# A mixture-of-experts layer that scatters widened token rows into expert order, lets the experts scatter their results, and moves the shared expert forward

## The chip, the cores and the metric

One core of one Trainium2 chip. The time is the device time of one launch, in microseconds, of the slowest (here the only) core; it is compared as the median of several runs. Beside the runs there is one profiled execution with a trace.

## The reference, cut to what matters

A two-layer transformer on 2 x 1024 tokens of 256 features, float32. Layer 0 is attention (16 heads) and a quantized gated feed-forward; layer 1 is retention (4 heads) and a mixture of experts, and only the latter is changed in what it does:

```python
router_logits = x @ gate_w.T
probs = jax.nn.softmax(router_logits, axis=-1)
topk_w, topk_idx = jax.lax.top_k(probs, K)            # E = 64 experts, K = 6, inner width 176
topk_w = topk_w / jnp.sum(topk_w, axis=-1, keepdims=True)
h = jax.nn.silu(jnp.einsum('th,eih->tei', x, experts_w1))
y = jnp.einsum('tei,ehi->teh', h, experts_w2)
routed_out = jnp.einsum('teh,te->th', y, combine)     # combine: the six weights, zero elsewhere
g, u = jnp.split(x @ shared_gate_up.T, 2, axis=-1)
shared_out = jax.nn.silu(g) * u @ shared_down.T       # inner width 352
return (routed_out + shared_out).reshape(orig_shape)
```

after which comes x = layernorm(x + ffn(x)).

## The kernel before, in words

The program is a row of blocks, each closed by a barrier of all engines: `attend`, `out_ffn` (output projection, feed-forward of layer 0, and on SyncE the weights and tables of the retention), `retention`, then `route`, `experts` and `combine`. Inside a block each engine has its own instruction stream, and semaphores order them. A stream is run in its written order, so an instruction that waits holds everything behind it on its engine.

`route`. `keep_x` holds the 2048 tokens as 16 tiles of 128 tokens, `keep_x_t` the transposed copy. TensorE makes the logits; VectorE takes the eight best, forms the six weights, counts tokens by expert, and gives each of the 12,288 (token, choice) pairs a slot in an array of 160 tiles of 128 slots, in which each expert begins a new tile (`slot_i`, L1563). SyncE copies `keep_x` to `x_rows` in HBM. Then the slots are inverted: for each of 96 (tile, choice) pairs VectorE and GpSimd make one-hot matrices (L1573 to L1576, L1458) and TensorE adds up their product (L1490), and the sum is `tok_i`, the token of each slot (L1581). A slot that no pair has comes out as token 0. `owner` is the expert of each tile (for tiles past the last used one the last expert).

`experts`. For each of the 160 tiles: GpSimd gathers 128 rows of 1 KB from `x_rows` by `tok_i` (L1624, ten buffers); SyncE loads the tile's expert (`exp_w`, 2 x 176 KB, six buffers); TensorE transposes the rows (L1638), ScalarE copies them (L1678), TensorE multiplies by the first weights (L1649), ScalarE applies silu (L1685), TensorE multiplies by the second (L1658), VectorE copies the result out (L1713), and ScalarE's queue writes the tile to `y_rows` (L1690), in slot order.

`combine`. For each token tile and choice GpSimd gathers 128 rows of `y_rows` by `slot_i` (L1757, 12 buffers), and VectorE adds them to `keep_x`, each times its weight (L1822). Meanwhile the shared expert is computed (L1773 on TensorE, L1801, L1812, L1783), its result is added (L612), and the layer norm follows in four chunks of four tiles (L620 to L640), each then stored to `out`.

## Time and profile before

| | |
|---|---|
| median of 3 runs | 1465.17 us (1461.19 to 1465.23) |
| the profiled execution, its own time | 1456.11 us |
| its span, first to last instruction | 1454.4 us |
| TensorE busy | 1185.9 us (82%) |
| VectorE busy | 818.7 us (56%) |
| GpSimd busy | 550.8 us (38%) |
| ScalarE busy | 520.6 us (36%) |
| DMA moved | 154.78 MB, mean 106 GB/s |

The shares are over the whole span, over stages with different limits; the blocks concerned begin at about 822 us (`route`), 936 us (`experts`) and 1299 us (`combine`) of the span. The time outside the span is 1.7 us. The profiled execution was 9 us shorter than the median of the runs.

### The profile page before, as it was taken

To read this page: it belongs to the slowest core of one execution; us is meant where nothing else is said; L and a number is where in the kernel's file an instruction comes from. 1 tells how busy PE (TensorE), PEld (TensorE's weight loads), DVE (VectorE), ACT (ScalarE), POOL (GpSimd) and SP (SyncE) were. 2 spreads that over 40 slices of the span, in tenths; PEclk is the share of its full clock that TensorE was granted. 3 is DMA by queue.
4 is the path that set the end of the run, shared out by engine and by line. 5 is a ranking of instruction groups with operands and counts; after the bars stand their busy time and mean duration, and the time that the engine had idled before them with its cause. 6 is when DMAs were issued, how large, how long until landed. Compare 5 with 4: busy or idle time off the path is not lost. (4 is left out here: it accounts for less than half of the span.)

```text
span 1454.4 us, 19589 instructions
## 1 busy us (share of the span) xinstructions
PE 1185.9 (82%) x6248; PEld 689.2 (47%) x6287; DVE 818.7 (56%) x1572; ACT 520.6 (36%) x1052; POOL 550.8 (38%) x564
## 2 busy tenths in 40 slices
PE   5589999999999699989997515699999997778641
PEld 2242222222222255665455511188888886664321
DVE  6499999999997565333446379712221221114554
ACT  1137777777778432101234100033333332221000
POOL 6002447663536500012110105454444443314775
PEclk9799999999999889989998755589999999888855
DMA  4960531443101400000000100199999999962343
GB/s 133 182 151 8 91 46 21 52 58 45 21 10 16 166 2 1 0 1 1 1 1 1 60 0 1 33 295 303 313 306 305 308 302 231 220 192 57 101 127 97
DMA packets 142584, 154.78 MB, mean 106 GB/s; under 512 B 50674, under 2 KB 111443, under 8 KB 142419
## 3 DMA queue, kind: packets, MB, share of 16 engines
q1 hardware_dynamic: 106882, 98.71, 26.9%
q0 software_dynamic: 12288, 33.57, 9.2%
q10 hardware_dynamic: 23312, 21.24, 4.5%
q8 instruction: 52, 0.85, 0.3%
q14 instruction: 50, 0.40, 0.1%
HBM read 118.34 MB, written 32.51 MB: 104 GB/s over the span
## 5 line engine op out<-in xcount | busy, mean ns | idle before, releaser
L495 ACT ACTIVATE l_ret_store<-attn_st 128x512 f32<-128x512 f32 x512 | 280.0, 598 | 103.5 <-PE attn_st L406 87.3
L519 DVE TENSOR_REDUCE attn_neg<-attn_mx 128x8 f32<-128x1024 f32 x256 | 299.1, 1202 | 13.0 <-PE attn_mx L386 12.1
L1713 DVE COPY exp_y_sb<-exp_y_ps 128x256 f32<-128x256 f32 x160 | 68.0, 425 | 288.7 <-PE exp_y_ps L1658 288.7
L1624 POOL DMA_INDIRECT exp_rows<-x_rows,moe_tok_i x160 | 150.9, 943 | 189.2 <-PE exp_xt_ps L1638 172.6
L1649 PE MATMUL exp_h_ps<-exp_xt,exp_w 128*88 128x128 f32 x1280 | 174.2, 281 | 23.2 <-DMA exp_w<-in_w 22.8
L386 PE MATMUL attn_mx<-attn_k_st,attn_q_st 96*128 96x512 bf16 x512 | 154.9, 384 | 17.8 <-DVE attn_neg L519 15.1
L1658 PE MATMUL exp_y_ps<-exp_w,exp_ht 96*128 96x256 f32 x640 | 167.9, 385 | 0.0
L1649 PEld LDWEIGHTS exp_h_ps<-exp_xt,exp_w 128*88 128x88 f32 x1280 | 150.3, 161 | 32.2 <-DMA exp_w<-in_w 31.1
L406 PE MATMUL attn_st<-attn_q_st,attn_k_st 128*128 128x512 bf16 x473 | 160.0, 383 | 5.3 <-ACT l_ret_store L495 2.3
L418 PE MATMUL attn_o<-l_ret_store,l_ret_tab 128*32 128x512 f32 x1024 | 136.4, 604 | 2.8 <-ACT l_ret_store L495 0.8
L1678 ACT ACTIVATE exp_xt<-exp_xt_ps 128x256 f32<-128x256 f32 x160 | 61.5, 384 | 210.4 <-PE exp_xt_ps L1638 206.8
L406 PEld LDWEIGHTS attn_st<-attn_q_st,attn_k_st 128*128 128x128 bf16 x512 | 48.1, 97 | 157.2 <-ACT l_ret_store L495 114.6
L1757 POOL DMA_INDIRECT comb_got<-y_rows,moe_slot_i x96 | 92.6, 965 | 78.3 <-POOLq L58 33.1
L1658 PEld LDWEIGHTS exp_y_ps<-exp_w,exp_ht 96*128 96x128 f32 x640 | 110.9, 193 | 9.2
L1685 ACT ACTIVATE exp_ht<-exp_h_ps 88x256 f32<-88x256 f32 x160 | 60.8, 380 | 114.6 <-PE exp_h_ps L1649 114.6
L278 POOL CAST attn_neg_parts<-attn_neg 128x128 bf16<-128x128 f32 x16 | 4.6, 290 | 209.1 <-DVE attn_neg L519 209.1
L386 PEld LDWEIGHTS attn_mx<-attn_k_st,attn_q_st 96*128 96x128 bf16 x512 | 48.5, 98 | 67.6 <-DVE attn_neg L519 29.5
L1822 DVE SCALAR_TENSOR_TENSOR keep_x<-comb_got,moe_weight,keep_x 128x256 f32<-128x256 f32 x96 | 46.6, 486 | 42.4 <-DMA comb_got<-y_rows,moe_slot_i 38.9
L1638 PE MATMUL exp_xt_ps<-keep_ident,exp_rows 128*128 128x128 f32 x320 | 63.1, 279 | 6.8 <-DVE exp_w L1708 6.0
L1490 PE MATMUL route_m<-route_hot_high,route_hot_low 128*128 128x320 bf16 x96 | 42.2, 447 | 26.8 <-DVE route_hot_high L1576 22.1
L354 PE MATMUL attn_st<-keep_x_t,l0b_front 128*128 128x512 f32 x64 | 37.1, 741 | 32.4 <-DVE l0b_front L505 25.1
L1783 PE MATMUL comb_y<-comb_w_down,comb_sh_h 128*128 128x256 f32 (+1 forms) x96 | 33.8, 510 | 35.4 <-DVE keep_x L612 35.4
(233 smaller groups left out, 1643.9 us busy)
## 6 DMA issues: line engine op xcount, KB each, us to landing
exp_w<-in_w SPq DMA_DIRECT2D x320, 176.0 KB
y_rows<-exp_y_sb ACTq DMA_DIRECT2D x160, 128.0 KB, 6.2
parts<-l0b_front SPq DMA_DIRECT2D x32, 192.0 KB, 11.3
attn_k_st<-parts SPq DMA_DIRECT2D x48, 128.0 KB, 7.2
attn_q_st<-parts SPq DMA_DIRECT2D x48, 128.0 KB, 7.9
l_ret_tab<-in_tables SPq DMA_DIRECT2D x4, 1024.0 KB
exp_rows<-x_rows,moe_tok_i POOLq DMA_INDIRECT x160, 6.3
keep_x_t<-in_x_t SPq DMA_DIRECT2D x4, 512.0 KB
```

What stands on the lines that cost most here:

```text
L386: mm = pe.matmul(bank[:, half * CH:(half + 1) * CH], q, k_st[g % BUFS][0:STACK, h, half * CH:(half + 1) * CH], start=True, stop=True)
L406: pe.matmul(st_ps[n % BANKS][:], k_st[g % BUFS][:, h, kt * P:(kt + 1) * P], q_st[g % BUFS][:, h, c * CH:(c + 1) * CH], start=True, stop=Tr ...
L418: mm = pe.matmul(o_ps[32 * h:32 * h + 32, :], v_st[:, b, kt, head + h], probs[s % 2][:, h], start=True, stop=True)
L495: act.activation(probs[s % 2][:, h], st_ps[n % BANKS][:], ACT.Exp, scale=SCALE0).then_inc(exp_done, 1)
L519: dve.tensor_reduce(neg[m % 2][:, i], mx_ps[slot["score", n] % 2][:].rearrange("p (j k) -> p j k", k=P), AX.X, ALU.max, negate=True).then_ ...
L1624: pool.indirect_dma_start(rows[b % RB][:], None, a["x_rows"], bass.IndirectOffsetOnAxis(ap=tok_i[:, b:b + 1], axis=0)).then_inc(rows_in[b ...
L1638: mm = pe.transpose(xt_ps[b % 2][:, k * P:(k + 1) * P], rows[b % RB][:, k * P:(k + 1) * P], ident[:])
L1649: mm = pe.matmul(h_ps[b % 2][0:HALF, j * P:(j + 1) * P], w1[n][:, k, j], xt[b % 2][:, k], start=(k == 0), stop=(k == KT - 1))
L1658: mm = pe.matmul(y_ps[b % 2][:, 0:E], ht[b % 2][:, j], w2[b % B][:, j], start=(j == 0), stop=(j == 1))
L1678: act.activation(xt[b % 2][:], xt_ps[b % 2][:, 0:KT * P].rearrange("p (k t) -> p k t", k=KT), ACT.Copy).then_inc(xt_in, 1)
L1713: dve.tensor_copy(y_sb[b % YB][:], y_ps[b % 2][:, 0:E]).then_inc(y_in, 1)
L1757: pool.indirect_dma_start(got[n % B][:], None, a["y_rows"], bass.IndirectOffsetOnAxis(ap=slot_i[:, t, k:k + 1], axis=0)).then_inc(got_in[n ...
```

## The change

`keep_x` gets rows of 276 numbers, 1104 bytes: the token's 256 features (`x` is a view of them), its number, its six slots, its six weights, six constants k x 2048 and one unused. What each block does now:

- `out_ffn`: GpSimd fills `pad`, a row that carries a token number far out of bounds and slots of -1, and SyncE writes it to all 20,480 rows of `xs` in HBM, in 8 transfers, behind the loads for the retention; the block ends only when they have landed.
- `route`: the one-hot products and `tok_i` are gone, and so is the copy to `x_rows`. GpSimd scatters each token tile's wide rows to `xs` once for each choice, by `slot_i`, 96 indirect transfers of 128 rows of 1104 bytes, and waits for all. The shared expert is computed here, on TensorE behind the slot arithmetic, and left in `moe_shared`.
- `experts`: the rows of a tile are contiguous in `xs`, and ScalarE's queue loads them (12 buffers, 11 tiles ahead). For each four tiles VectorE finds in the rows which of the six slots is this one (`aim`: four small operations), and from that the weight of the row and the row of `y_rows` that it goes to: choice x 2048 + token. VectorE multiplies by the weight as it copies the result out of PSUM, and GpSimd scatters 128 rows of 1 KB to `y_rows`; padding rows have a destination out of bounds and are not written. For the first 16 tiles VectorE also adds `moe_shared` to `keep_x`.
- `combine`: SyncE loads for each token tile its six rows a token, 768 KB in one plain transfer, 8 buffers. For even tiles VectorE adds them in halves; for odd ones TensorE does, as six products with the identity into one PSUM bank. No weights and no gathers are left.

The diff, cut to its core:

```diff
@@ out_ffn
+            sp.wait_ge(padded, 3)
+            for i in range(PAD_PARTS):
+                sp.dma_start(a["xs"].rearrange("(b p) n -> p b n", p=P)[:, i * PER_PAD:(i + 1) * PER_PAD],
+                             pad[:].unsqueeze(1).to_broadcast([P, PER_PAD, XW])).then_inc(pad_out, 16)
+            sp.wait_ge(pad_out, 16 * PAD_PARTS)
@@ route, SyncE
-            sp.dma_start(a["x_rows"].rearrange("(t p) n -> p t n", p=P), x[:]).then_inc(x_out, 16)
+            sp.dma_start(w_up[:], a["w_sh_up"].rearrange("(k p) n -> p k n", p=P)).then_inc(sh_in, 16)
...
@@ route, GpSimd
-            pool.wait_ge(split, 1)
-            for n, (t, k) in list(enumerate(pairs))[1::2]:
...
-                pool.tensor_scalar(hot_low[:, n % HOTS], iota[:, 0:P], low[:, t, k:k + 1], None,
-                                   ALU.is_equal).then_inc(hot_low_in, 1)
+            pool.wait_ge(slotted, 1)
+            for t, k in pairs:
+                pool.indirect_dma_start(a["xs"], bass.IndirectOffsetOnAxis(ap=slot_i[:, t, k:k + 1], axis=0),
+                                        wide[:, t], None, bounds_check=TILES * P - 1, oob_is_err=False
+                                        ).then_inc(rows_out, 16)
+            pool.wait_ge(rows_out, 16 * len(pairs))
@@ route, TensorE
-            for n, (t, k) in enumerate(pairs):
...
+            for c in range(NCH + 1):
+                if c < NCH:
+                    for m in range(ST):
+                        shared_up(c * ST + m)
+                if c >= 1:
+                    for t in range((c - 1) * TC, c * TC):
+                        shared_down(t)
@@ route, VectorE
+            dve.tensor_copy(slot_i[:], slot).then_inc(slotted, 1)
+            for n in range(NCH * ST):
...
+                dve.tensor_tensor(sh_h[c % 2][0:rows, m], u_ps[n % 2][0:rows, :], sh_gate[n % 2][0:rows],
+                                  ALU.mult).then_inc(fuse, 1)
@@ experts, GpSimd
-                pool.indirect_dma_start(rows[b % RB][:], None, a["x_rows"], bass.IndirectOffsetOnAxis(
-                    ap=tok_i[:, b:b + 1], axis=0)).then_inc(rows_in[b % RB], 16)
+                pool.wait_ge(y_in, b + 1)
+                pool.wait_ge(aimed, b // SET + 1)
+                pool.indirect_dma_start(a["y_rows"], bass.IndirectOffsetOnAxis(
+                    ap=dst_i[b // SET % 6][:, b % SET:b % SET + 1], axis=0), y_sb[b % YB][:], None,
+                    bounds_check=TOP * TOK - 1, oob_is_err=False).then_inc(y_out[b % YB], 16)
@@ experts, ScalarE
-                act.dma_start(a["y_rows"].rearrange("(t p) n -> t p n", p=P)[b], y_sb[b % YB][:]
-                              ).then_inc(y_out[b % YB], 16)
+                act.dma_start(rows[:, b % RB], a["xs"].rearrange("(b p) n -> b p n", p=P)[b]
+                              ).then_inc(rows_in[b % RB], 16)
@@ experts, VectorE
+                if b % SET == 1 and b // SET + 1 < TILES // SET:
+                    aim(b // SET + 1)
+                if b < NT:
+                    dve.tensor_tensor(x[:, b], x[:, b], shared[:, b], ALU.add).then_inc(shared_in, 1)
...
-                dve.tensor_copy(y_sb[b % YB][:], y_ps[b % 2][:, 0:E]).then_inc(y_in, 1)
+                dve.tensor_scalar(y_sb[b % YB][:], y_ps[b % 2][:, 0:E], weight[b // SET % 4][:, b % SET, 0:1], None,
+                                  ALU.mult).then_inc(y_in, 1)
@@ combine, SyncE
+            for t in range(NT):
+                if t >= B:
+                    sp.wait_ge(norm["summed"], t - B + 1)
+                sp.dma_start(got[t % B][:], a["y_rows"].rearrange("(k t p) n -> t p k n", k=TOP, p=P)[t]
+                             ).then_inc(got_in[t % B], 16)
@@ combine, TensorE
+            for t in range(1, NT, 2):
+                pe.wait_ge(got_in[t % B], 16 * (t // B + 1))
+                if t >= 5:
+                    pe.wait_ge(norm["summed"], t - 3)
+                for k in range(TOP):
+                    mm = pe.matmul(y_ps[t // 2 % 2][:, 0:E], keep["ident"][:], got[t % B][:, k],
+                                   start=(k == 0), stop=(k == TOP - 1))
+                mm.then_inc(made, 1)
@@ combine, VectorE
+            def sum_rows(t):
+                n, rows = t // 2, got[t % B]
+                dve.wait_ge(got_in[t % B], 16 * (t // B + 1))
+                dve.tensor_tensor(rows[:, 0:3], rows[:, 0:3], rows[:, 3:6], ALU.add).then_inc(halved, 1)
+                dve.wait_ge(halved, n + 1)
+                dve.tensor_tensor(rows[:, 0], rows[:, 0], rows[:, 1], ALU.add).then_inc(paired, 1)
+                dve.tensor_tensor(x[:, t], x[:, t], rows[:, 2], ALU.add).then_inc(thirds, 1)
...
```

GpSimd's own stream from the end of `route` to the end of the program, before (line, operation, what it writes and reads, shape, count):

```order
L1453 MEMSET route_sums 128x64
L1458 TENSOR_SCALAR route_hot_low<-route_iota,route_low 128x128 x48
L1624 DMA exp_rows<-x_rows,moe_tok_i 128x256 x160
L1757 DMA comb_got<-y_rows,moe_slot_i 128x256 x48
```

and the same stream of the changed kernel:

```order
L1479 MEMSET route_sums 128x64
L1482 DMA xs<-keep_x,route_slot_i 20480x276 x96
L1679 IOTA exp_mine 128x160
L1684 DMA y_rows<-exp_y_sb,exp_dst_i 12288x256 x160
L648 TENSOR_TENSOR comb_ln_rstd<-comb_ln_var,keep_neg_half 128x4 x4
```

The 96 indirect transfers have moved from `combine` (where they were gathers, 48 of them in the row shown and 48 more behind it) to `route`, where they are scatters; the 160 of `experts` have turned from gathers ahead of the tile to scatters behind it.

ScalarE's stream in `experts`, in the steady state before (silu, then the write of the tile two back):

```order
L1678 ACTIVATE exp_xt<-exp_xt_ps 128x256
L1685 ACTIVATE exp_ht<-exp_h_ps 88x256
L1690 DMA y_rows<-exp_y_sb 128x256
```

and of the changed kernel, from the start of the block:

```order
L1738 DMA exp_rows<-xs 128x276 x11
L1745 ACTIVATE exp_xt<-exp_xt_ps 128x256 x2
L1738 DMA exp_rows<-xs 128x276
L1752 ACTIVATE exp_ht<-exp_h_ps 88x256
```

Eleven loads now stand ahead of ScalarE's first copy, and in each tile the transfer stands between the copy and the silu instead of behind the silu.

## Rows read from the trace of the kernel before

**Rows 1.** The windows view by stage: busy us of each engine, granted clock, DMA.

```profile
core 0: us, PE busy (x) PEld busy (x) DVE busy (x) ACT busy (x) POOL busy (x), PEclk, DMA share, GB/s
...
884.00:936.00 52.00, 42.16 (x96) 9.94 (x96) 50.18 (x245) 0.00 (x0) 29.34 (x48) 0.50 0.00 1
...
1040.00:1080.00 40.00, 39.83 (x281) 35.94 (x280) 8.49 (x20) 15.24 (x40) 18.82 (x20) 1.00 0.98 306
...
1200.00:1240.00 40.00, 29.34 (x188) 25.26 (x186) 5.95 (x14) 10.65 (x28) 13.17 (x14) 0.96 1.00 229
...
1380.00:1420.00 40.00, 16.52 (x40) 9.96 (x40) 23.90 (x64) 0.59 (x1) 30.64 (x33) 0.59 0.44 127
```

**Rows 2.** VectorE's copies of the experts' results in the timeline: first, 121st, last.

```profile
951.51 0.42 DVE L1713 COPY exp_y_sb<-exp_y_ps 128x256 f32<-128x256 f32 x1 [11.93 <-PE exp_y_ps L1658]
...
1195.98 0.42 DVE L1713 COPY exp_y_sb<-exp_y_ps 128x256 f32<-128x256 f32 x1 [1.53 <-PE exp_y_ps L1658]
1197.94 0.42 DVE L1713 COPY exp_y_sb<-exp_y_ps 128x256 f32<-128x256 f32 x1 [1.54 <-PE exp_y_ps L1658]
...
1295.85 0.42 DVE L1713 COPY exp_y_sb<-exp_y_ps 128x256 f32<-128x256 f32 x1 [0.44 <-PE exp_y_ps L1658]
```

**Rows 3.** DMA queues, 936 to 1190 us: q1 weights, q0 gathers, q10 writes.

```profile
q1 hardware_dynamic: 29424, 43.64, 53.4%
q0 software_dynamic: 6155, 16.82, 23.0%
```

**Rows 4.** The same queues, 1245 to 1290 us.

```profile
q1 hardware_dynamic: 4392, 6.52, 48.3%
q0 software_dynamic: 528, 1.44, 24.2%
```

**Rows 5.** The timeline of GpSimd's gathers in `combine`: the first two and the last.

```profile
1299.76 0.94 POOL L1757 DMA_INDIRECT comb_got<-y_rows,moe_slot_i  x1 [33.07 <-POOLq L58]
1301.00 0.94 POOL L1757 DMA_INDIRECT comb_got<-y_rows,moe_slot_i  x1 [0.30 <-issue]
...
1438.81 0.95 POOL L1757 DMA_INDIRECT comb_got<-y_rows,moe_slot_i  x1 [0.30 <-issue]
```

**Rows 6.** DMA issues of 1340 to 1440 us: KB each, median us to landing.

```profile
comb_got<-y_rows,moe_slot_i POOLq DMA_INDIRECT x77, 2.8
```

**Rows 7.** The timeline of `route`'s end: start us, us, what, idle before it.

```profile
883.05 0.21 DVE L1563 CAST moe_slot_i<-route_slot 128x96 int32<-128x96 f32 x1
...
934.40 0.24 DVE L1581 CAST moe_tok_i<-route_tok_f 128x160 int32<-128x160 f32 x1
935.79 0.55 DVE L1708 MEMSET exp_ht<- 96x256 f32 x2 [1.14 <-PEq L58]
```

**Rows 8.** Groups of `combine` by line: busy us, mean ns, idle before.

```profile
L1783 PE MATMUL comb_y<-comb_w_down,comb_sh_h 128*128 128x256 f32 (+1 forms) x96 | 33.8, 510 | 35.4 <-DVE keep_x L612 35.4
L1773 PE MATMUL comb_g<-keep_x_t,comb_w_up 128*128 128x512 f32 (+1 forms) x48 | 26.4, 677 | 10.6 <-DMA comb_w_down<-in_w_sh_down 10.6
L1773 PE MATMUL comb_u<-keep_x_t,comb_w_up 128*128 128x512 f32 (+1 forms) x48 | 25.1, 649 | 7.3 <-DVE comb_sh_h L1812 7.3
```

**Rows 9.** DMA in 820 to 833 us, GB/s of 40 slices, and its issue.

```profile
GB/s 0 0 0 0 0 0 0 0 0 0 0 214 190 331 337 336 329 331 337 350 356 353 350 353 347 353 350 350 347 350 328 47 25 25 19 0 0 0 0 0
...
x_rows<-keep_x SPq DMA_DIRECT2D x1, 2048.0 KB
```

**Rows 10.** DMA in 490 to 640 us, 40 slices of 3.75 us, GB/s.

```profile
GB/s 143 271 372 416 392 18 4 0 0 0 0 0 0 4 0 0 0 0 0 0 4 0 0 0 2 0 0 0 4 0 0 0 0 0 0 4 0 0 0 0
```

**Rows 11.** Groups of 833 to 884 us: VectorE on 128x1024 float32.

```profile
L1561 DVE TENSOR_TENSOR route_pick<-route_place,route_chosen 128x1024 f32<-128x1024 f32 x6 | 7.4, 1226 | 0.2
```

**Rows 12.** The timeline of `combine`'s end, and a pair of its sums on TensorE.

```profile
1427.51 2.93 PE L1783 MATMUL comb_y<-comb_w_down,comb_sh_h 128*128 128x256 f32 x6 [4.17 <-DVE keep_x L612]
...
1442.10 0.42 DVE L612 TENSOR_TENSOR keep_x<-comb_y,keep_x 128x256 f32<-128x256 f32 x1
1442.44 1.39 DVE L620 BATCH_NORM_STATS2 comb_ln_stats<-keep_x 128x6 f32<-128x256 f32 x4
```

316 lines of the change are left out of this document (154 added, 162 removed).

## The prediction

> **What bounds the kernel now.** I first read the windows view by stage [rows 1]. No one engine bounds the three blocks that change. At the end of `route` (884 to 936 us) VectorE is busy 50.18 of 52 us and TensorE 42.16: they build and multiply the one-hot matrices. In `experts` TensorE is busy 39.8 of 40 us at the full clock while the DMA share is 0.98 at 306 GB/s, so two resources run out almost together. From 1200 us the rate falls: 14 tiles in 40 us instead of 20, TensorE 29.3 busy, DMA share 1.00 but only 229 GB/s. In `combine` GpSimd has the largest share, 30.64 of 40 us, at a DMA share of 0.44.
>
> Then the tile rhythm of `experts` in the timeline [rows 2]. The usual step from one result to the next is 1.96 us, which is TensorE's own pace. The first 120 steps take (1195.98 - 951.51) = 244.5 us, 2.04 each; the last 39 take 99.9 us, 2.56 each. The queues tell why. In the steady part the gathers hold 23.0% of 16 engines for 254 us for 16.82 MB [rows 3], 57 ns for each 1 KB row; in 1245 to 1290 us 24.2% of 16 x 45 us for 1.44 MB [rows 4], 124 ns for each. The weights cost 50 and 53 ns a KB. So only the gathers are slow there. What the late tiles have in common is that no token belongs to them: 12,288 pairs fill about 130 of 160 tiles, and each empty slot gathers token 0. I take 128 reads of one row as the cause of the late stalls.
>
> Last, `combine` [rows 5]: gathers start 1.25 us apart (0.94 us of GpSimd and 0.30 between), 96 of them from 1299.76 to 1438.81; a transfer lands 2.8 us after its issue [rows 6]. The loop is GpSimd's issue rate, with 17 us of start-up in which it waits for the shared expert.
>
> **`route`: what goes and what comes.** The slots are ready at 883.05 + 0.21 = 883.3 us, and `experts` begins at 935.8 [rows 7]; 52.5 us lie between. In their place stand 96 scatters on GpSimd. No scatter is in the trace. The nearest row is the gather: the same engine, the same 128 indices, the same count of rows, so 1.25 us each. I take it: 883.4 + 95 x 1.25 + 0.95 = 1003.1, the last lands some 2 us later, and 1.15 us of barrier as in [rows 7] follow. `experts` begins at about 1006: **70 us later**. The lower bound is an issue without the gap, 0.95 us each, 29 us less. The upper bound is a scatter that has to land before the next is issued, 1.25 + 2.8 us, 270 us more. I stay near the gather, and allow it up to 0.2 us more for the bounds test and the 1104-byte row, 19 us.
>
> Beside it runs the shared expert. Its matmuls were busy 33.8 + 26.4 + 25.1 = 85.3 us [rows 8], part of it at the low clock. TensorE can start when the slots' base is known, and VectorE joins at 883.3, so it ends by about 883 + 85 + 10 for the single output bank = 978, under the scatters. It costs nothing, but if the scatters were cheaper than 1.0 us each it would be the bound: without that cover the block would still be 43 us longer.
>
> **`out_ffn`.** The padding rows are 20,480 x 1104 B = 22.6 MB. A 2 MB store of 1 KB rows ran at about 345 GB/s [rows 9], so 66 us. They queue behind loads that end near 512 us, and from then to 640 the DMA engines move nothing [rows 10]: they are done at about 580, and the block has 60 us to spare. The three small fills ahead of GpSimd's first product cost under 1 us where its next norm waits anyway. Zero; uncovered it would be 66 us.
>
> **`experts`.** Bytes a tile before: 352 KB weights + 128 gathered + 128 written = 608 KB, at 306 GB/s 2.03 us, just the 2.04 of the first 120 steps. Now: 352 + 138 loaded + 12,288 / 130 = 94 rows written, 94 KB = 584 KB, 1.95 us, and TensorE needs 1.96. Late tiles: 352 + 138 KB from distinct addresses and nothing written, 1.6 us, so TensorE's 1.96. Both movements go in one direction. I keep a few stalls and take 1.98 us for all 159 steps: 314.8 against 344.3 us, **29 us less**. The bounds: 1.96 gives 33 less; tail or stalls unchanged gives 5 to 0 less.
> On the other engines a tile has slack. GpSimd's scatter of 0.94 us needs only `y_in`. VectorE's copy is 0.42 us in 1.96; the four small operations of `aim` come once in four tiles, and the addition of 0.42 us in 16 tiles. What they could delay is the copy out of a PSUM bank that has a twin. ScalarE issued one transfer a tile and still does, but its load is ahead of the silu, which `down` waits for; the copy ahead of it ends over 1 us before `up` does, so 0.33 us fits. `aim` waits for rows up to six tiles on, loaded 11 ahead. If it waited, VectorE's copies, then `y_ps`, then TensorE would be held.
>
> **`combine`.** It lasted 1454.4 - 1295.85 = 158.6 us from the last copy [rows 2]. Now 16 loads of 786 KB, 12.6 MB; at the 340 GB/s of a run of 1 KB rows [rows 9] 37 us, and 1.5 MB of stores among them 4.5 us. VectorE per pair: three rows at 3/4 of 1.23 us [rows 11] = 0.95, two additions and two norm additions of at most 0.42, with waits 2.6 us; with the norm of four tiles 8.4 us for four tiles, under the 10.6 of their transfers. So DMA sets the pace. Ahead of it: the last scatter and the barrier 4.5 us, the first transfer 2. Behind: six products at the low clock 2.93 us and their wait 3.2 us, then 1442.10 to 1454.4 unchanged, 12.3 us [rows 12]. Sum 4.5 + 2 + 37 + 4.5 + 3.2 + 12.3 = 63.5: **95 us less**. If VectorE were the bound it would be 34 for 41.5, 103 less.
> One thing speaks against 340 GB/s. A token's six rows lie 2 MiB apart, and the only rows in this trace with an address pattern that collides cost 124 instead of 57 ns [rows 3, 4]. At 2.2 times, the loads take 81 us, 44 more. The Trainium skill (DMA: Bandwidth & Descriptors, Latency and other measured facts) gives 164 GB/s where each partition's row is 2 MiB from the next, an estimate of 77 us for the loads; here the partitions' rows are adjacent and only the six blocks lie so far apart, which no row shows. [...]
>
> **Sum.** +70 - 29 - 95 = -54 us. The profiled execution had 1454.4 us of span and 1.7 around it, so 1402 by its measure; it was 9 us below the median of the runs, and against 1465.17 the same difference gives **1411 us**.
>
> **The rivals.**
> *A, the scatter is dear and the kernel slower.* One price decides: 54 us / 96 = 0.56, so from 1.81 us a scatter nothing is gained, and at 2.05 us it is 1434 + 54 = 1488. For it: the row is written, not read, is longer, and a bounds test is new. Against: the number of rows to describe is the same, and the DMA share is 0.35 to 0.44 during gathers, so there is room. A chance of 0.10.
> *B, the late tiles stay slow.* Then the stalls come from the repeated weights of the last expert, not from the gathers, and 25 us stay: 1436. Against: 50 to 53 ns a KB for weights. 0.08.
> *C, the loads of `combine` collide,* +44: 1455, faster by 0.7% still. 0.08.
> *D, the new order holds TensorE in `experts`* (rows late for `aim`, or ScalarE's transfer ahead of the silu): 0.2 us a tile is 32 us, 1443. For it: SyncE's issues there sometimes take longer. 0.10.
> *E, the change does not do what it says:* scatters cheaper by the gap, with the shared expert as bound, 1385. 0.04.
>
> **How the numbers follow.** The forecast, 1395 to 1427 with its own bounds (the 19 us of a slightly dearer scatter above, exact 1.96 and VectorE's pace below), has 0.60. The range goes up to take in B and D: 1394 to 1448. Faster, same and slower are parted at 0.3% of the time, about what a measurement of this kernel can tell. A is split into 0.02 near no change and 0.08 above; the rest is faster: 0.90, 0.02, 0.08.
>
> **What would show it.** GpSimd's scatters in `route` 1.25 us apart, near 883 to 1003, with the shared expert finished before them; steps of 1.96 us in `experts` up to the last tile; loads in `combine` landing 2.3 to 2.6 us apart with VectorE waiting for them. A scatter of 1.8 us, a shared expert that ends last, or VectorE waiting for rows in `experts` would make me wrong.

## The result and the profile after

The changed kernel takes 1472.91 us (median of 20 runs, 1467.42 to 1478.41), the kernel before beside it 1467.03 us (20 runs, 1460.09 to 1480.38). The ratio is 1.0044, its 95% interval 1.0027 to 1.0061: slower by 0.4%, where I had forecast 1411 us, 3.7% faster. The profiled execution took 1476.08 us, its span 1474.4.

The windows view of the changed kernel, in the columns of [rows 1]; first the end of `route` in three parts, then `experts`, then `combine`:

```profile
core 0: us, PE busy (x) PEld busy (x) DVE busy (x) ACT busy (x) POOL busy (x), PEclk, DMA share, GB/s
884.00:950.00 66.00, 36.55 (x78) 16.71 (x79) 3.90 (x6) 4.47 (x9) 50.19 (x52) 0.74 0.30 108
950.00:1010.00 60.00, 4.02 (x12) 2.46 (x10) 1.38 (x2) 1.57 (x3) 43.43 (x45) 0.55 0.30 108
1010.00:1051.00 41.00, 29.00 (x84) 17.05 (x84) 2.07 (x3) 6.00 (x14) 0.00 (x0) 0.82 0.00 0
1100.00:1140.00 40.00, 39.75 (x276) 35.45 (x277) 12.72 (x40) 14.94 (x40) 18.47 (x19) 1.00 0.95 291
1240.00:1280.00 40.00, 38.63 (x258) 33.01 (x258) 12.24 (x39) 13.90 (x37) 18.43 (x19) 1.00 0.95 274
1420.00:1460.00 40.00, 24.34 (x84) 18.88 (x84) 23.50 (x67) 0.00 (x0) 4.16 (x3) 0.78 1.02 328
```

The second line is the surprise: from 950 to 1010 us GpSimd issues scatters, and all other engines stand still, TensorE with 4.02 us of work in 60. In the third line the scatters are over and the shared expert is still being computed.

The timeline of GpSimd's scatters and of the barrier behind them, which answers to [rows 5, 7]:

```profile
884.25 1.24 POOL L1482 DMA_INDIRECT xs<-keep_x,route_slot_i  x1 [58.13 <-DVE route_slot_i L1623]
885.80 0.97 POOL L1482 DMA_INDIRECT xs<-keep_x,route_slot_i  x1 [0.30 <-issue]
...
1005.88 0.97 POOL L1482 DMA_INDIRECT xs<-keep_x,route_slot_i  x1 [0.30 <-issue]
...
1050.08 0.38 ACT L1562 ACTIVATE moe_shared<-route_y 128x256 f32<-128x256 f32 x1 [1.65 <-PE route_y L1529]
...
1051.41 0.55 DVE L1792 MEMSET exp_ht<- 96x256 f32 x2 [16.21 <-PEq L74]
```

The scatters are as forecast, 1.28 us apart (0.97 and 0.30), 884.3 to 1006.9 us. But `experts` begins at 1051.4, 45 us after the 1006 of the forecast, behind ScalarE's last copy of the shared expert.

Why that was late shows in the timeline of TensorE, ScalarE and VectorE beside the scatters:

```profile
899.57 0.38 ACT L1562 ACTIVATE moe_shared<-route_y 128x256 f32<-128x256 f32 x1 [2.42 <-PE route_y L1529]
...
911.55 2.93 PE L1529 MATMUL route_y<-route_w_down,route_sh_h 128*128 128x256 f32 x6 [6.83 <-issue]
914.27 2.46 PE L1519 MATMUL route_g<-keep_x_t,route_w_up 128*128 128x512 f32 x4
916.56 1.88 PE L1519 MATMUL route_u<-keep_x_t,route_w_up 128*128 128x512 f32 x4
...
923.03 0.38 ACT L1562 ACTIVATE moe_shared<-route_y 128x256 f32<-128x256 f32 x1 [11.53 <-remote]
934.23 0.60 ACT L1558 ACTIVATE route_sh_gate<-route_g 128x512 f32<-128x512 f32 x1 [10.82 <-issue]
934.88 3.73 PE L1519 MATMUL route_g<-keep_x_t,route_w_up 128*96 128x512 f32 x4 [13.00 <-issue]
945.43 0.69 DVE L1631 TENSOR_TENSOR route_sh_h<-route_u,route_sh_gate 128x512 f32<-128x512 f32 x1 [46.46 <-DMA parts<-l0b_front]
...
1006.33 0.38 ACT L1562 ACTIVATE moe_shared<-route_y 128x256 f32<-128x256 f32 x1 [26.71 <-remote]
```

Read them crosswise. TensorE's output tile of 911.55 is complete by 914.5; ScalarE, which waits for nothing else, takes it at 923.03. The gate product of 914.27 is complete by 916.7 and taken at 934.23, the up product of 916.56 by 918.4 and taken at 945.43. The profile models the end of a product, but the trace also records when a semaphore rises. For the gate product that ended at 896.52, ahead of these, that is 896.54; for the output tile that ended at 914.48 it is 923.00, and for the gate product that ended at 920.16 it is 956.61. So it is not ScalarE that wakes up late: TensorE's completion signals arrive one at a time, 11.2 us apart, and further and further behind the work. In the other direction nothing is late: TensorE goes on at 934.88, right behind ScalarE's 934.23 + 0.60. The releasers named ("remote", a DMA of a much earlier block) are old semaphore events: none of them is what was waited for. The queues don't explain it, since the DMA share is 0.30.

The experts' results on VectorE (which answer to [rows 2]) and the queues of 250 us in `experts` (q1 weights, q10 rows, q0 scatters, to [rows 3]):

```profile
1067.10 0.48 DVE L1803 TENSOR_SCALAR exp_y_sb<-exp_y_ps,exp_weight 128x256 f32<-128x256 f32 x1 [10.63 <-PE exp_y_ps L1719]
...
1329.62 0.48 DVE L1803 TENSOR_SCALAR exp_y_sb<-exp_y_ps,exp_weight 128x256 f32<-128x256 f32 x1 [2.54 <-PE exp_y_ps L1719]
...
1409.60 0.48 DVE L1803 TENSOR_SCALAR exp_y_sb<-exp_y_ps,exp_weight 128x256 f32<-128x256 f32 x1 [0.38 <-PE exp_y_ps L1719]
```

```profile
q1 hardware_dynamic: 27829, 41.28, 57.3%
q10 hardware_dynamic: 16448, 16.15, 22.3%
q0 software_dynamic: 5413, 11.18, 13.8%
```

The last 39 steps take 80.0 us instead of 99.9, and no step over 3.3 us is left: the tail came out as forecast. The first 120 take 262.5 us, 2.19 each, instead of the 244.5 of before and the 1.98 of the forecast.

Last, `combine`: DMA in 1420 to 1462 us and the timeline of its edges, which answer to [rows 9, 12]:

```profile
GB/s 15 146 361 379 359 347 351 347 349 347 348 347 349 349 347 355 346 352 349 347 347 348 352 349 348 346 350 347 347 348 350 346 349 364 384 386 296 46 301 208
```

```profile
1411.27 0.97 POOL L1684 DMA_INDIRECT y_rows<-exp_y_sb,exp_dst_i  x1 [0.30 <-issue]
1419.84 8.17 SPq L1826 DMA_DIRECT2D comb_got<-y_rows  x6
1424.80 0.96 DVE L1858 TENSOR_TENSOR comb_got<-comb_got 128x768 f32<-128x768 f32 x1 [14.72 <-DMA comb_got<-y_rows]
...
1465.46 0.42 DVE L628 TENSOR_TENSOR keep_x<-comb_y,keep_x 128x256 f32<-128x256 f32 x1 [1.68 <-PE comb_y L1849]
```

It runs at the DMA rate, 347 GB/s, and takes 1474.4 - 1409.6 = 64.8 us, where 63.5 was forecast.

### The profile page after: what moved, and what is told of

Read it like the earlier page. It is cut to its first block and busy times, and to the rows that moved or that the text cites. A ratio compares the mean times of both kernels' runs of the same rounds, so it can differ in the third digit from the quotient of the medians.

```text
span 1474.4 us, 20063 instructions
## 1 busy us (share of the span) xinstructions
PE 1176.9 (80%) x6287; PEld 693.5 (47%) x6287; DVE 776.3 (53%) x1429; ACT 526.0 (36%) x1068; POOL 530.1 (36%) x522
## 5 line engine op out<-in xcount | busy, mean ns | idle before, releaser
L1684 POOL DMA_INDIRECT y_rows<-exp_y_sb,exp_dst_i x160 | 156.3, 977 | 204.4 <-DVE exp_y_sb L1803 82.4
L1803 DVE TENSOR_SCALAR exp_y_sb<-exp_y_ps,exp_weight 128x256 f32<-128x256 f32 x160 | 77.4, 484 | 241.2 <-PE exp_y_ps L1719 166.8
L422 PE MATMUL attn_st<-attn_q_st,attn_k_st 128*128 128x512 bf16 x512 | 173.5, 383 | 2.9 <-ACT l_ret_store L511 2.1
L402 PE MATMUL attn_mx<-attn_k_st,attn_q_st 96*128 96x512 bf16 x512 | 154.9, 384 | 15.6 <-DVE attn_neg L535 15.3
L1719 PE MATMUL exp_y_ps<-exp_w,exp_ht 96*128 96x256 f32 x640 | 164.6, 379 | 0.4 <-ACT exp_ht L1752 0.4
L1710 PEld LDWEIGHTS exp_h_ps<-exp_xt,exp_w 128*88 128x88 f32 x1280 | 145.5, 158 | 38.5 <-DMA exp_w<-in_w 26.8
L1482 POOL DMA_INDIRECT xs<-keep_x,route_slot_i x96 | 93.6, 975 | 87.1 <-DVE route_slot_i L1623 58.1
L1529 PE MATMUL route_y<-route_w_down,route_sh_h 128*128 128x256 f32 (+1 forms) x96 | 30.2, 459 | 75.9 <-issue 62.5
L1631 DVE TENSOR_TENSOR route_sh_h<-route_u,route_sh_gate 128x512 f32<-128x512 f32 (+1 forms) x12 | 8.2, 688 | 143.9 <-DMA parts<-l0b_front 89.9
L1082 PE MATMUL ret_a<-keep_x_t,l_ret_store 128*128 128x512 f32 x128 | 59.5, 618 | 2.4 <-PEq L74 2.4
```

The source lines that it names most:

```text
L402: mm = pe.matmul(bank[:, half * CH:(half + 1) * CH], q, k_st[g % BUFS][0:STACK, h, half * CH:(half + 1) * CH], start=True, stop=True)
L422: pe.matmul(st_ps[n % BANKS][:], k_st[g % BUFS][:, h, kt * P:(kt + 1) * P], q_st[g % BUFS][:, h, c * CH:(c + 1) * CH], start=True, stop=Tr ...
L1482: pool.indirect_dma_start(a["xs"], bass.IndirectOffsetOnAxis(ap=slot_i[:, t, k:k + 1], axis=0), wide[:, t], None, bounds_check=TILES * P - ...
L1684: pool.indirect_dma_start(a["y_rows"], bass.IndirectOffsetOnAxis(ap=dst_i[b // SET % 6][:, b % SET:b % SET + 1], axis=0), y_sb[b % YB][:], ...
L1710: mm = pe.matmul(h_ps[b % 2][0:HALF, j * P:(j + 1) * P], w1[n][:, k, j], xt[b % 2][:, k], start=(k == 0), stop=(k == KT - 1))
L1719: mm = pe.matmul(y_ps[b % 2][:, 0:E], ht[b % 2][:, j], w2[b % B][:, j], start=(j == 0), stop=(j == 1))
```

## The experiments

All edits are to the changed kernel unless said otherwise. Runs of one group had the same chip. "Indirect" means the last scatter's end in `route`, "shared" the shared expert's last copy, "experts" that block's first instruction, all in us of the span; "steps" are the mean of the first 120 steps of `experts`, and the sum of the last 39; "before" is the kernel before on that chip. All columns are of one execution each, but for the last two of e10_pause and e5b_lockstep: there the times are medians of 6 and 8 executions, beside 13 of the kernel before. These spread over 7.7, 5.5 and 15.0 us, so a difference between two single times can be trusted only if it is larger.

| run | indirect | shared | experts | steps | kernel | before |
|---|---|---|---|---|---|---|
| profile after | 1006.9 | 1050.5 | 1051.4 | 2.19, 80.0 | 1476.1 | |
| e1_throttle | 1009.9 | 1056.2 | 1057.2 | 2.14, 77.1 | 1472.2 | 1471.5 |
| e2_after | 1008.3 | 1085.2 | 1086.1 | 2.17, 80.2 | 1507.2 | |
| e3_aligned | 1008.8 | 1053.5 | 1054.5 | 2.16, 78.5 | 1471.8 | |
| e4_owner | 1011.2 | 1057.0 | 1057.9 | 2.15, 82.1 | 1478.5 | |
| e5_lockstep | 1017.2 | 950.5 | 1027.7 | 2.13, 79.2 | 1442.9 | 1451.9 |
| e6_gather | 1138.2 | 952.3 | 1150.2 | 2.17, 80.4 | 1573.8 | |
| e7_drain | 1034.4 | 954.4 | 1044.9 | 2.12, 79.6 | 1459.2 | |
| x4_direct | 1010.9 | 953.3 | 1021.4 | 2.17, 82.0 | 1444.3 | |
| c0_before | | | | 2.07, 96.4 | 1475.3 | 1472.4 |
| c1_after | 1008.8 | 1055.7 | 1056.7 | 2.14, 77.9 | 1472.4 | |
| x1_nowrite | 1009.5 | 1056.0 | 1057.0 | 2.09, 80.7 | 1468.7 | |
| e8_loose | 1020.5 | 987.2 | 1031.0 | 2.13, 77.1 | 1444.8 | |
| c2_after | 1009.6 | 1055.6 | 1056.6 | 2.15, 80.0 | 1474.6 | 1465.2 |
| x4b_direct | 1008.3 | 1051.3 | 1052.2 | 2.16, 79.9 | 1470.7 | |
| e6b_gather | 1136.1 | 1168.6 | 1169.8 | 2.15, 79.1 | 1589.2 | |
| e9_tight | 1019.5 | 969.5 | 1030.1 | 2.17, 78.5 | 1450.0 | |
| e10_pause | 1017.9 | 950.5 | 1028.4 | 2.13, 80.4 | 1446.4 | 1469.3 |
| e5b_lockstep | 1026.9 | 980.8 | 1037.4 | 2.17, 78.0 | 1458.5 | |

### First group: how many scatters are outstanding, and the experts' rows

```diff
+                if n >= 4:
+                    pool.wait_ge(rows_out[n % 4], 16 * (n // 4))
```

> Edit: of the route's 96 scatters at most four are outstanding (GpSimd waits for scatter n-4 before it issues scatter n). In the changed kernel's profile the scatters run from 884.2 to 1005.9 us, one every 1.28 us, and from 903 us on TensorE's completion signals reach ScalarE and VectorE one by one, 11.2 us apart, so that the block ends at 1051.3 us. Theory 1 (what holds the signals back is the number of scatters that are outstanding, or that GpSimd's sequencer has run ahead and its queue is full): no signal is late, the shared expert ends by about 960 us, the block ends 5 to 10 us behind the last scatter, at 1010 to 1020 us, and the whole kernel takes 1435 to 1445 us. Theory 2 (each scatter holds signals back by itself, however many are outstanding): the signals stay about 11 us apart and the block ends at 1045 to 1060 us. Rival (the chip needs the depth): the scatters themselves slow down to 2 us or more each and the block ends after 1070 us.

The block ended at 1057.2 us and the signals came 11.2 and 22.4 us apart as before. The scatters kept their 1.28 us: four were hardly ever outstanding in the unlimited loop either (in x4_direct below one lands 2.5 us after its issue). Theory 1 fell: the signals are late although no more than four transfers are under way.

```diff
             pe.wait_ge(sh_in, 16 * (1 + ST))
+            pe.wait_ge(rows_out, 16 * len(pairs))
```

> Edit: TensorE starts the shared expert only when all 96 scatters have landed. Theory (scatters and the shared expert disturb each other, alone each is as quick as its rows say): the scatters end at 1006 us as before the edit, the shared expert then takes 24 groups of four matmuls at 1.72 us and 16 output tiles at 2.04 us, about 74 us, with no late signal, and the block ends near 1081 us; the kernel takes about 30 us more than the changed one. Rival (the shared expert is slow by itself, since its operands or its weights are slow to read): signals are late after 1006 us too and the block ends after 1120 us.

The shared expert alone took 1008.3 to 1085.2, 77 us, with no late signal, and the scatters alone were no quicker than beside it. The two disturb each other in one direction: the scatters hold up the shared expert.

```diff
+PITCH = 320
-    a["xs"] = nc.dram_tensor("xs", (TILES * P, XW), F32, kind="Internal").ap()
+    a["xs"] = nc.dram_tensor("xs", (TILES * P, PITCH), F32, kind="Internal").ap()
```

> Edit: the widened rows lie 1280 bytes apart in HBM instead of 1104, so that each begins at a multiple of 256 bytes; as many bytes are moved as before, and the scatters of the route have no bounds check. Theory A (the experts' 160 steps of 2.15 us instead of 1.98 come from reads of 1104-byte rows that begin anywhere, which take 61 ns each): the rows' reads fall below 55 ns each and the experts take 335 to 345 us from their first instruction to the last copy instead of 358. Theory B (the queue of the weights is what the tiles wait for, at 55 ns a kilobyte, whatever the rows' place): the experts take 355 to 361 us. The route doesn't change by more than 3 us by either.

First to last copy of the experts' results took 337.6 us, which lies among the 334.2 of e1_throttle and the 340.4 of e2_after on the same chip, with untouched experts. Where a row begins makes no difference that these runs can tell.

```diff
+            chain(dve.tensor_scalar(spare[:], owner_f[:], float(EXPERTS), None, ALU.is_ge))
+            chain(dve.tensor_scalar(other[:], tile_no[:], float(-TILES), None, ALU.add))
...
+            chain(dve.tensor_tensor(owner_f[:], owner_f[:], other[:], ALU.add))
```

> Edit: the tiles behind the last one in use name experts 0, 1, 2 ... as their owners instead of all naming the last expert, so that no tile reads the weights that its neighbour has just read; their rows are pads, so nothing else changes. Theory of the forecast's second rival (weights of one expert read again and again are slow): the queue of the weights takes less than 57 ns a kilobyte in the tail instead of 58.9, and the experts end 5 us or more earlier. Theory B (all reads compete for the same bandwidth, wherever they lie): no difference over 3 us in the experts' time of 358.2 us.

The last 39 steps took 82.1 us, the longest of the group. Weights that are read again and again aren't slow; what rival B wanted as a cause isn't there in the changed kernel.

### Second group: signals paced, gathers, pauses, direct stores

```diff
+                if n >= 4 and n % 2 == 0 and 9 + n // 2 < len(signals):
+                    pool.wait_ge(*signals[9 + n // 2])
```

> Edit: from the fifth scatter on, before every second scatter, GpSimd waits for TensorE's next completion signal of the shared expert (29 of its 40 signals, one behind the other), so that no signal can fall more than two scatters behind; behind scatter 60 the rest run unhindered. With four outstanding scatters the signals were as late as without a limit, so it isn't the number outstanding. Theory 3 (TensorE's signal loses to GpSimd's stream of scatters and passes as soon as GpSimd pauses): the shared expert ends by about 970 us, the scatters end between 1010 and 1025 us, the block by 1030 us, and the kernel takes 1445 to 1455 us. Rival (a signal needs 11.2 us once the stream has begun, whether GpSimd pauses or not): 29 signals at up to 11 us make the block end after 1100 us.

```diff
+            for n, (t, k) in enumerate(pairs):
+                if n >= RD:
+                    pool.wait_ge(read_in[n % RD], 16 * (n // RD))
+                pool.indirect_dma_start(read[:, n % RD], None, a["xs"], bass.IndirectOffsetOnAxis(
...
```

> Edit: ahead of its 96 scatters GpSimd issues 96 gathers by the same indices, of the same rows of 1104 bytes, from the rows' array into 24 spare buffers; the shared expert has its place, so it now runs beside the gathers. Theory 4 (the late signals belong to scatters, that is to indirect transfers that write HBM): the shared expert runs at its pace beside the gathers and ends near 945 us; the gathers end near 1008 us, the scatters near 1132 us, and the block right behind them. Theory 3 (any stream of indirect transfers at this pace does it): the signals come 11 us apart beside the gathers too, and again beside the scatters, so that the shared expert has not ended by 1050 us.

```diff
+                if n and n % 8 == 0:
+                    pool.wait_ge(rows_out, 16 * n)
```

> Edit: after every eight scatters GpSimd waits until all that it has issued have landed, then goes on: eleven pauses of about 2 us. Theory 3 (a signal passes as soon as GpSimd pauses, and the stream has to run some 20 us before signals are late at all): the shared expert ends by 960 us, the scatters near 1030 us, the block with them, and the kernel takes 1450 to 1460 us. Rival (the lateness has nothing to do with the stream's breaks): signals stay 11.2 us apart and the block ends after 1065 us.

```diff
-                pool.indirect_dma_start(a["y_rows"], bass.IndirectOffsetOnAxis(
...
+                pool.dma_start(a["y_rows"].rearrange("(t p) n -> t p n", p=P)[b % (TOP * NT)], y_sb[b % YB][:]
+                               ).then_inc(y_out[b % YB], 16)
```

> Edit in the experts, which leaves out the scatter of the results: each tile's 128 rows of 1 KB are stored in order by one direct transfer from GpSimd's queue, pads too, as in the kernel before. Its output is not that of the reference. Theory C (the scatter of 1 KB rows to places all over 12 MB is what makes all queues slower per kilobyte, 55 ns for the weights instead of 49.7): the weights' queue falls to 51 ns a kilobyte or less, and the experts take 335 to 345 us from their first instruction to the last copy instead of 358.2. Theory D (the rows' direct reads, or the bytes as a whole, do it): the experts take 350 to 365 us.

None of the four had a late signal, and each seemed to bear a theory out. But x4_direct has the route of the changed kernel, word for word, and was free of them too: its shared expert ended at 953.3 us, its block at 1021.4. This was a chip on which the kernel before takes 1451.9 us. The group tells nothing about signals without a control. It does show the route undisturbed: behind the last scatter `experts` still begins 10.5 us later, not 3. In the trace's records of GpSimd 7.9 us of that are the drain that ends its block. On the experts, theory C fell: with direct stores the first 120 steps took 2.17 us, with scatters in the other three 2.12 to 2.17.

### Third group: the controls

> The kernel before, unchanged, profiled on the same chip as the three below, since its time differs by 20 us from chip to chip (1471.5 us beside the first four runs, 1451.9 us beside the next four), and the profiles of before and after weren't necessarily taken on one. If the experts' steps of the kernel before are quicker than those of the changed one on one chip too, by 0.1 us or more, then the change itself slows them; if both have steps of about the same length, the difference in the two profiles lay in the chips.

> The changed kernel, unchanged, as the control that the last four runs lacked: one of them had the route of the changed kernel word for word, and still its shared expert ended at 953 us with no late signal and its block at 1021 us. Theory 5 (the late signals belong to the program: its layout or its timing): this run shows them again, the shared expert ends at 1045 to 1057 us and the experts begin behind it. Theory 6 (they depend on the chip or the execution): this run may show none, the shared expert then ends near 953 us, the block near 1021 us, and the kernel takes about 30 us less than in its first profile, beside before.

The late signals were back in c1_after (shared expert ended at 1055.7 us). And they were in the kernel before as well: in its `combine`, which took 172.0 us here from the last copy instead of 158.6. The timeline of c0_before there, TensorE and ScalarE:

```profile
1353.54 1.88 PE L1773 MATMUL comb_g<-keep_x_t,comb_w_up 128*96 128x512 f32 x4
1353.65 0.60 ACT L1801 ACTIVATE comb_sh_gate<-comb_g 128x512 f32<-128x512 f32 x1 [4.47 <-DMA y_rows<-exp_y_sb]
...
1370.45 0.59 ACT L1801 ACTIVATE comb_sh_gate<-comb_g 96x512 f32<-96x512 f32 x1 [16.20 <-DMA y_rows<-exp_y_sb]
```

The product of 1353.54 is complete by 1355.4 and taken at 1370.45, 16.8 us after the one ahead of it. GpSimd's gathers ran from 1336.5 to 1366.5 there. The profile of before that I had read has a longer stretch without a pause, 36 gathers from 1331.3 to 1376.9 us, and no late signal in it; 42 us into it ScalarE still takes a product as it ends:

```profile
1371.91 1.88 PE L1773 MATMUL comb_g<-keep_x_t,comb_w_up 128*128 128x512 f32 x4
1373.83 0.60 ACT L1801 ACTIVATE comb_sh_gate<-comb_g 128x512 f32<-128x512 f32 x1 [2.84 <-PE comb_g L1773]
```

The queues of 250 us, c0_before from 952 us, 4.5 ahead of its first copy (q0 gathers, q10 stores), and c1_after from its first copy (q10 rows, q0 scatters):

```profile
q1 hardware_dynamic: 28929, 42.92, 53.9%
q0 software_dynamic: 5768, 15.76, 22.9%
q10 hardware_dynamic: 16750, 15.25, 18.9%
```

```profile
q1 hardware_dynamic: 28337, 42.04, 57.7%
q10 hardware_dynamic: 16707, 16.41, 22.5%
q0 software_dynamic: 5536, 11.37, 13.9%
```

```diff
-                    bounds_check=TOP * TOK - 1, oob_is_err=False
+                    bounds_check=0, oob_is_err=False
```

> Edit in the experts: the bounds of the result scatter are set so low that all rows but those for place 0 are dropped; the array is filled with zeros earlier, beside the pads. The output is not that of the reference. Theory E (weights, rows and results compete for one bandwidth, and what is above 1.96 us a step is the weights' lateness): without the 44 MB/s-class writes, 11.2 MB in 254 us, the steps fall to 1.96 to 2.03 us, and the experts take 320 to 330 us from first to last copy. Rival (reads alone are the limit, writes are free): the steps stay at 2.10 us or more and they take 334 us or more.

The queues of x1_nowrite, 250 us from the first copy, in which nearly nothing is written:

```profile
q1 hardware_dynamic: 28958, 42.95, 66.6%
q10 hardware_dynamic: 17103, 16.79, 24.5%
q0 software_dynamic: 5667, 0.07, 1.5%
```

Add the reads: 42.92 + 15.76 = 58.7 MB in c0_before, 42.04 + 16.41 = 58.5 in c1_after, 42.95 + 16.79 = 59.7 in x1_nowrite, 235, 234 and 239 GB/s, while 15.3, 11.4 and 0.1 MB were written. Taking all writes away gives 0.05 us a step; the steps of 2.09 us and the 331.6 us from first to last copy lie between what theory E and its rival wanted, the steps nearer to the rival. So it isn't the sum of both directions that sets the pace. That the bytes read set it is argued and not shown: a tile reads the same bytes in any of these kernels but for 10 KB, so like steps give like read rates whatever the cause, and reads alone run at 347 GB/s in `combine`. (The expectation's 11.2 MB in 254 us are 44 GB/s, not MB/s.)

```diff
+                if n >= 12 and n % 2 == 0 and 4 + n // 2 < len(signals):
+                    pool.wait_ge(*signals[4 + n // 2])
```

> Edit: as with the signals waited for one by one before every second scatter, but beginning at scatter 12 and seven signals behind, so that no wait holds unless a signal is really late. If the chip or execution shows late signals in the unchanged kernel here, this kernel shows whether such a bound is enough: shared expert ended by 970 us, last scatter by 1012 us, block by 1023 us. If the unchanged kernel has no late signals either, this one's route ends within 2 us of that one's.

Here one sees how a pause works. The timeline of e8_loose:

```profile
943.29 1.88 PE L1526 MATMUL route_u<-keep_x_t,route_w_up 128*128 128x512 f32 x4
943.85 0.97 POOL L1489 DMA_INDIRECT xs<-keep_x,route_slot_i  x1 [0.30 <-issue]
946.65 0.60 ACT L1565 ACTIVATE route_sh_gate<-route_g 128x512 f32<-128x512 f32 x1 [5.28 <-DMA parts<-l0b_front]
947.30 1.96 PE L1526 MATMUL route_g<-keep_x_t,route_w_up 128*96 128x512 f32 x4 [2.13 <-ACT route_sh_gate L1565]
947.40 0.97 POOL L1489 DMA_INDIRECT xs<-keep_x,route_slot_i  x1 [2.58 <-DMA parts<-l0b_front]
948.67 0.97 POOL L1489 DMA_INDIRECT xs<-keep_x,route_slot_i  x1 [0.30 <-issue]
948.80 0.69 DVE L1638 TENSOR_TENSOR route_sh_h<-route_u,route_sh_gate 128x512 f32<-128x512 f32 x1 [20.70 <-DMA parts<-l0b_front]
```

GpSimd stops at 944.8 for a signal that is late. Within 1.9 us ScalarE has its own, and the others follow at once; no further 11 us pass. The kernel took 1444.8 us, 28 less than the control, though the shared expert ended at 987 and not by 970.

### Fourth group: chip or program, scatter or gather

> The changed kernel, unchanged, as the control of the three below on their chip. Two profiles of it have shown the late signals (shared expert ended at 1050.5 and 1055.7 us), on chips where the kernel before takes about 1470 us; four other kernels on a chip where that takes 1452 us showed none. If the lateness goes with the chip, this run shows it where the kernel before takes 1465 us or more here, and not where it takes 1455 us or less.

> The kernel whose experts store their results directly, again: its route is that of the changed kernel, word for word, and had no late signal on the chip where the kernel before took 1451.9 us. If the chip decides (theory 6), its shared expert ends within 5 us of the control's, whichever that is. If the program decides (theory 5: what GpSimd's queue holds behind the scatters, or where its code lies), it ends at 953 us while the control's ends near 1050 us.

Control 1055.6 us, x4b_direct 1051.3: the same kernel that had no late signal two groups before has them here. It goes with the chip, or with a condition of it, not with the program.

One thing in the traces goes with it too: how many rises of semaphores they record. Of four kernels there are two traces each. Where all signals are prompt they hold 21,323 (the profile before), 21,580 (e5_lockstep), 21,603 (x4_direct) and 23,144 (e6_gather); where some are late 15,860 (c0_before), 17,524 (e5b_lockstep), 20,283 (x4b_direct) and 17,290 (e6b_gather). Records are missing in every trace but the profile before and the four of the second group. So a rival stands untested: the recording itself may take part in the lateness. Against it speaks only that the cost isn't in the profiled executions alone. All 20 times of the changed kernel lie at 1467 us or more, where x4_direct, with prompt signals and the same route, took 1444.3; but what was recorded in the other 19 isn't known.

> 96 gathers ahead of the 96 scatters, again, with a control beside it. If the control's signals are late and this one's aren't while its gathers run (shared expert ended near 952 us), scatters hold signals back and gathers don't. If this one's are late too, any unbroken stream of indirect transfers does it. If the control's aren't late either, the run tells nothing on it.

The timeline of e6b_gather while only gathers were issued (884.8 to 1009 us):

```profile
957.35 0.59 ACT L1568 ACTIVATE route_sh_gate<-route_g 96x512 f32<-96x512 f32 x1 [21.80 <-DMA attn_wq<-wj]
985.35 0.38 ACT L1572 ACTIVATE moe_shared<-route_y 128x256 f32<-128x256 f32 x1 [27.41 <-issue]
1002.15 0.38 ACT L1572 ACTIVATE moe_shared<-route_y 128x256 f32<-128x256 f32 x1 [16.42 <-remote]
```

Gathers do it as well as scatters (theory 4 fell), and the shared expert ended at 1168.6 us, behind both loops. Between the first two rows lies a signal that VectorE took at 968.55, 11.2 us behind the first; from there the output tiles come 16.8 us apart, 1.5 times 11.2.

```diff
+                if n >= 6 and n % 3 == 0 and 1 + n * 2 // 3 < len(signals):
+                    pool.wait_ge(*signals[1 + n * 2 // 3])
```

> Edit: from scatter 6 on GpSimd waits before every third scatter for the signal that TensorE reaches by then at its own pace (two signals for three scatters), so that on its way it never waits unless a signal is late, and a late one is let through by that very pause. Expected where signals are late in the control: shared expert ended by 965 us, last scatter issued by 1013 us, block ended by 1024 us (10.5 us behind the last scatter, of which GpSimd's draining takes 7.9), kernel 28 to 35 us shorter than the control. Rival (a pause must be long, or releases one signal only after 11 us): block ended after 1035 us.

Shared expert 969.5, block 1030.1, 24.7 us less than the control: the pauses release, but four were needed, after the scatters issued at 910.5, 933.0, 958.6 and 965.6 us, of which three stand 22 and 26 us apart: lateness comes back about as long after a pause as it needs after the start.

### Fifth group: pauses on a clock, and timed

```diff
+                if n in (10, 20, 30, 40, 50):
+                    pool.wait_ge(rows_out, 16 * n)
```

> Edit: ahead of scatters 10, 20, 30, 40 and 50 GpSimd waits until all that it has issued have landed: pauses of about 2 us, 13 us apart, while the shared expert runs. In the runs with late signals the first came 16 to 20 us after the stream began or went on again. Theory 7 (a stream of under 15 us holds nothing back): no late signal, shared expert ended by 955 us, last scatter issued by 1018 us, block ended at 1024 to 1030 us, kernel 25 us or more faster than before where before takes 1470 us. Rival (the lateness comes back whatever the stream's length): shared expert ended after 985 us; the block still ends with the scatters, near 1030 us, unless it ends after them.

> The kernel that waits for one signal before every second scatter, again and timed, since its first run was on a chip where the changed kernel's own route may have had no late signal. One pause of 9 us at scatter 4; then signal and scatter go side by side with two to five signals of slack. Expected by theory 3 (a pause releases a signal): shared expert ended by 970 us, block by 1035 us, the kernel 1440 to 1450 us, 1.3 to 2 per cent faster than before. Rival: more pauses than the first and a block that ends after 1040 us.

The timeline of one pause of e10_pause:

```profile
896.99 0.97 POOL L1484 DMA_INDIRECT xs<-keep_x,route_slot_i  x1 [0.30 <-issue]
900.24 0.97 POOL L1484 DMA_INDIRECT xs<-keep_x,route_slot_i  x1 [2.28 <-DMA xs<-keep_x,route_slot_i]
...
1016.89 0.97 POOL L1484 DMA_INDIRECT xs<-keep_x,route_slot_i  x1 [0.30 <-issue]
1028.24 1.80 ACTq L1740 DMA_DIRECT2D exp_rows<-xs  x4
```

Five pauses of 2 us and not one late signal: the shared expert ended at 950.5 us, as on the undisturbed chip, while in e5b_lockstep on the same chip ScalarE waited 9.9 and 7.3 us for output tiles of TensorE, and the shared expert ended at 980.8. So signals are late on this chip too, and a stream broken every 13 us avoids it (theory 7). e10_pause takes 1446.42 us against 1469.3: ratio 0.9848, interval 0.9815 to 0.988. e5b_lockstep 1458.47 us: 0.9924, 0.9900 to 0.9949, outside the 1440 to 1450 expected. e10_pause is the change with its main fault mended, and the faster of the two that were timed over several executions.

## Why the prediction was wrong

Against its own profile the forecast was 1402 us, and 1476.1 came: 74 us too many, 45.4 in `route` (1051.4 for 1006), 27 in `experts` (358.2 us from its first instruction to the last copy instead of 360.1, where 29 less was forecast), 1.3 in `combine`.

**The scatters, right.** Forecast 1.25 us each up to 1003.1; measured 1.28 up to 1006.9, 3.8 us more with the start 0.9 us later. Rival A had no part in it.

**"Beside it runs the shared expert... It costs nothing", the step that failed.** The work was sized well enough: 77 us alone in e2_after, and finished at 950 to 954 us wherever signals are prompt, even earlier than the forecast 978. What failed is that two engines with nothing in common in the program leave each other alone. Beside GpSimd's unbroken stream TensorE's signals came late, as they did not where the stream was absent (e2_after) or broken (e10_pause), and the shared expert ended last. With the 10.5 us behind the scatters of the undisturbed runs the block would have ended at 1017.4; the late signals cost 1051.4 - 1017.4 = 34 us. I had named "a shared expert that ends last" as what would make me wrong, but only by its own work, and gave it no price on that side. The trace that I read had the same pair of streams in `combine`, where gathers and shared expert got on without a late signal for 46 us, so I had no row against the step; another profile of the same kernel, c0_before, would have had one. Which of the two I had read was chance.

**The barrier behind the scatters, mis-sized.** I took 2 us of landing and the 1.15 of [rows 7], where GpSimd had issued no transfers; it takes 10.5 behind 96 of them, 7.9 of which are GpSimd's drain. 7.6 us too few (with 3.8 and 34 the 45.4 of the block), hidden in the changed kernel by the late signals and open in e10_pause. In front of `combine` the same: 4.5 us forecast, 10.2 from last copy to first load; there the shorter rest made up for it.

**"608 KB, at 306 GB/s", the second step that failed.** It counted reads and writes together and gained from fewer bytes in all. x1_nowrite shows that such a sum doesn't set the pace: it was 296 GB/s in c0_before at 2.07 us a step and 239 here at 2.09. Reads alone were at 235 GB/s in c0_before, and each tile now reads 352 + 138 instead of 352 + 128 KB. At that rate 490 KB (502,000 bytes) take 2.13 us, near the 2.14 measured; by this account, which no run shows, the change could only make the first 120 steps longer. On one chip they went from 2.07 to 2.14 us, 8.8 us in all. The bytes read would explain 2 of those 3.5%; the rest is open: without writes most of it is gone (2.09), but direct stores, which write more, don't add to it (2.16 in x4b_direct, 2.15 in its control).

**The tail, right in time.** 80.0 us instead of the forecast 77, stalls gone, though the changed kernel still reads the last expert's weights again and again, and e4_owner, which doesn't, is no quicker: rival B is out. (My 50 and 53 ns a KB for the weights were for 1000 bytes; for 1024, as with the gathers, they are 50.9 and 54.6. Nothing rests on it.) That 128 reads of one row had made the stalls fits, since they are all that the tail has lost beside its writes, but no run brought them back alone. On one chip the experts gained 344.9 - 335.2 = 9.7 us from first to last copy, not 29.

**`combine` and the padding, right.** The padding rows were written at 340 GB/s and done by about 575 us, `retention` began at 647.9 instead of 648.5 us, and the first scatter stood 0.9 us behind its forecast: nothing of their 66 us shows. Rival C didn't come: six blocks 2 MiB apart are read at 347 GB/s. The rule of the Trainium skill (DMA: Bandwidth & Descriptors, Latency and other measured facts) speaks of partitions that lie so far apart, which no run here has. Rival D didn't come either: of the 9.5 us that TensorE's first product waits in c1_after from 1080 to 1330 us, 7.6 end with a load of weights, none with rows.

**The sum.** Without the late signals the kernel is faster than before, as e10_pause shows, by 22.9 us and not by 54. `experts` gives 19 us less than forecast, the pauses cost 10, the barrier 7.6, the scatters 3.8, `combine` 1.3; about 13 us of these 42 come back if the kernel before has late signals too on such chips, as its `combine` had in c0_before (172.0 us for 158.6, one profile each). That leaves 2 us without an account.

## What to carry to other kernels

Beside a loop of indirect transfers on GpSimd that runs some 16 us without a pause, what TensorE has to tell the other engines can come late, in four of the five groups of runs here. Break such a loop every ten transfers while TensorE's results are waited for, and look in a profile for results that are taken in steps of 11.2 us while the engine that made them had long been done. Count reads and writes apart when a stage is near its DMA rate: here taking nearly all writes away gave 0.05 us a step. And before a group of edits is read as a proof, run the unchanged kernel beside it: four edits "worked" here on a chip that never had the fault.

## What the runs showed of the hardware

- TensorE's signals 11.2 us apart (also 16.8 and 22.4 for steps that need more than one) under an unbroken stream of indirect transfers, in either direction, with at most four outstanding too, beginning 16 to 20 us after the stream. A pause of GpSimd of 2 us, every ten transfers, keeps them prompt. One of five groups of runs and the profile before didn't show it; only in their traces are the records of semaphores complete. What holds the signals, and whether the recording takes part, is open; VectorE's and ScalarE's own signals were prompt throughout.
- GpSimd's drain at the end of a block of indirect transfers: 7.9 us behind 96 in a row, 4.8 us behind `experts`.
- After such waits TensorE is granted its lower clock (0.55 of full speed on average in the changed kernel from 950 to 1010 us, with 4 us of work in 60), so the shared expert's rest is slow as well: in e8_loose and e9_tight, at a granted clock of 0.50, its last output tiles came 3.40 us apart, in e10_pause, at 1.00, 2.04.
